# Local attention in six layers: a new order of the TensorE, ScalarE, VectorE and GpSimd steps of a turn

## What is computed

```
for i in range(6):
    q, k, v = split(shift_tokens(x) @ Wqkv[i])              # 16 heads of 64
    q, k = rotary(l2norm(q) * qs), rotary(l2norm(k) * ks)
    sim = q @ k^T * 8, windows of 32 tokens, each looks at itself and the one before
    x = x + (softmax(sim) @ v) @ Wo[i]
    a, gate = split(layernorm(shift_tokens(x)) @ W1[i] + b1[i])
    x = x + (a * gelu(gate)) @ W2[i] + b2[i]
```

## Time and profile before

| what | value |
|---|---|
| median of 3 runs | 2087.13 us (2086.69 to 2090.17) |
| profiled execution, its own time | 2087.44 us |
| its span, first to last instruction | 2085.6 us |
| TensorE busy | 1895.0 us, 91% of the span |
| GpSimd busy | 1445.9 us, 69% |
| VectorE busy | 1446.0 us, 69% |
| ScalarE busy | 1395.4 us, 67% |

### The profile page before, as it was taken

How to read it: one execution, slowest core, us unless ns; L and a number is a source line. 1 busy time by engine, 2 the same in 40 slices (tenths; PEclk the granted TensorE clock), 3 DMA queues, 4 the chain that set the end, 5 groups by cost and what they waited for, 6 DMA issues and landing times. The chain is left out here.

```text
span 2085.6 us, 77661 instructions
## 1 busy us (share of the span) xinstructions
PE 1895.0 (91%) x32069; PEld 1312.6 (63%) x32069; DVE 1446.0 (69%) x2609; ACT 1395.4 (67%) x2781; POOL 1445.9 (69%) x1837
## 2 busy tenths in 40 slices
PE   5648999999999999999999999999999999669958
PEld 4526666666666666666666666666666666456648
DVE  2357687778776877777777867787778786245546
ACT  1157777787777777777777777777787777235425
POOL 1158887888788878887788778877888787112334
PEclk9779999999999999999999999999999999769969
DMA  2011131111311113111113111121111111030002
GB/s 96 0 34 48 48 96 45 46 48 46 95 46 48 46 46 96 48 48 55 40 41 102 55 40 36 41 81 31 30 33 31 30 30 33 2 99 1 18 30 76
DMA packets 67088, 99.85 MB, mean 48 GB/s; under 512 B 15367, under 2 KB 51608, under 8 KB 65970
## 3 DMA queue, kind: packets, MB, share of 16 engines
q1 hardware_dynamic: 65234, 91.72, 15.3%
q0 software_dynamic: 1504, 3.17, 0.4%
HBM read 44.50 MB, written 21.45 MB: 32 GB/s over the span
## 5 line engine op out<-in xcount | busy, mean ns | idle before, releaser
L1074 PE MATMUL b_bank_proj<-layer_weights,b_stream_t 128*128 128x512 f32 x1152 | 589.4, 613 | 34.0 <-DVE b_plain_moved L948 17.9
L948 DVE TENSOR_TENSOR b_plain_moved<-b_bank_proj,b_rope 128x1024 f32<-128x1024 f32 x384 | 464.0, 1219 | 191.8 <-ACT b_squares L834 137.8
L759 POOL TENSOR_TENSOR b_rotated<-b_plain_moved 128x1024 f32<-128x1024 f32 x192 | 453.5, 2362 | 23.1 <-DVE b_plain_moved L948 18.7
L774 POOL TENSOR_TENSOR b_rotated<-b_rotated,b_inv_norm 128x1024 f32<-128x1024 f32 x192 | 365.2, 1902 | 15.6
L834 ACT ACTIVATE b_squares<-b_bank_proj 128x512 f32<-128x512 f32 x384 | 229.1, 597 | 116.1 <-PE b_bank_proj L1074 111.6
L865 ACT ACTIVATE b_k_t<-b_bank_shared 64x512 f32<-64x512 f32 x384 | 226.5, 590 | 119.9 <-PE b_bank_shared L1082 117.4
L1074 PEld LDWEIGHTS b_bank_proj<-layer_weights,b_stream_t 128*128 128x128 f32 x1152 | 186.9, 192 | 136.1 <-issue 45.7
L779 POOL TENSOR_TENSOR b_probs<-b_probs,b_inv_sum 128x512 f32<-128x512 f32 x192 | 200.3, 1044 | 90.1 <-DVE b_inv_sum L969 88.7
L856 ACT ACTIVATE b_q_t<-b_bank_shared 64x512 f32<-64x512 f32 x384 | 225.7, 588 | 34.3 <-PE b_bank_shared L1082 31.4
L1082 PE MATMUL b_bank_shared<-const_tables,b_rotated 128*128 128x128 f32 x1536 | 233.1, 277 | 15.6 <-POOL b_rotated L774 15.2
L1101 PEld LDWEIGHTS b_bank_scores<-b_k_t,b_q_t 128*32 128x32 f32 x12288 | 184.5, 111 | 98.9 <-issue 95.8
(11 more groups left out here) (320 smaller groups left out, 2866.8 us busy)
## 6 DMA issues: line engine op xcount, KB each, us to landing
b_v_shifted<-b_v SPq DMA_DIRECT2D x96, 384.0 KB, 3.5
sorted_rows<-constants SPq DMA_DIRECT2D x135, 129.0 KB, 3.4
layer_weights<-L_ffn_Wqkv SPq DMA_DIRECT2D x6, 1536.0 KB
b_v_shifted<-b_v SPq DMA_DIRECT2D x72, 128.0 KB, 3.4
layer_weights<-L_ffn_w SPq DMA_DIRECT2D x16, 256.0 KB, 5.2
layer_weights<-L_ffn_Wo SPq DMA_DIRECT2D x6, 512.0 KB
c_sorted_in<-sorted_rows SPq DMA_DIRECT2D x23, 129.0 KB, 2.1
layer_weights<-L_ffn_W SPq DMA_DIRECT2D x6, 341.0 KB
```

Of the source, the lines that this page charges most:

```text
L759: nc.gpsimd.tensor_tensor(out=turned[:, k, :], in0=pm[:, k, 0, :], in1=pm[:, k, 1, :], op=ALU.add).then_inc(add_done, 1)
L774: nc.gpsimd.tensor_tensor(out=tk, in0=tk, in1=repeat_last(rn[:, k, :], DH), op=ALU.mult).then_inc(rope_done, 1)
L948: nc.vector.tensor_tensor(to, src.to_broadcast(shape), tab.to_broadcast(shape), ALU.mult).then_inc(mul_done, 1)
L1074: nc.tensor.matmul(out, xs[:, b, t * P:(t + 1) * P], w, start=True, stop=True).then_inc(proj_full, 1)
```

## The change

All four lists are replaced; no code outside them differs. Over the 24 turns each engine does the same steps as before. Counted over the whole walk, no step of TensorE or ScalarE moves by more than five places, none of VectorE by more than three, none of GpSimd by more than two. The lists are also cut at another place of the turn, which alone moves nothing. From the diff (TensorE's list, and the stretches of the others that matter):

```
 PE_TURN
-    ("project", 1, 4), ("project", 1, 5), ("scores", 0, 0), ("probs_t", -1, 1), ("project", 2, 0),
-    ("project", 2, 1), ("pv", -1, 0), ("heads_t", 1, 0), ("project", 2, 2), ("heads_t", 1, 1), ("scores", 0, 1),
-    ("leave", -2, 0), ("project", 2, 3), ("out", -1, 0), ("heads_t", 1, 2), ("heads_t", 1, 3), ("back", -1, 0),
-    ("project", 2, 4), ("project", 2, 5), ("probs_t", 0, 0), ("scores", 1, 0), ("project", 3, 0),
-    ("heads_t", 2, 0), ("project", 3, 1), ("probs_t", 0, 1), ("scores", 1, 1), ("project", 3, 2), ("pv", 0, 0),
-    ("heads_t", 2, 1), ("norm_t", -1, 0), ("project", 3, 3), ("heads_t", 2, 2), ("up", -1, 0), ("heads_t", 2, 3),
-    ("out", 0, 0), ("up", -1, 1), ("enter", 1, 0), ("probs_t", 1, 0), ("scores", 2, 0), ("up", -1, 2),
-    ("up", -1, 3), ("project", 3, 4), ("probs_t", 1, 1), ("project", 3, 5), ("heads_t", 3, 0), ("project", 4, 0),
-    ("project", 4, 1), ("pv", 1, 0), ("heads_t", 3, 1), ("project", 4, 2), ("scores", 2, 1), ("out", 1, 0),
+    ("project", 2, 0), ("project", 2, 1), ("heads_t", 1, 0), ("probs_t", -1, 1), ("scores", 0, 0), ("pv", -1, 0),
+    ("heads_t", 1, 1), ("project", 2, 2), ("scores", 0, 1), ("project", 2, 3), ("heads_t", 1, 2), ("leave", -2, 0),
+    ("out", -1, 0), ("project", 2, 4), ("heads_t", 1, 3), ("project", 2, 5), ("back", -1, 0), ("project", 3, 0),
+    ("probs_t", 0, 0), ("scores", 1, 0), ("heads_t", 2, 0), ("probs_t", 0, 1), ("project", 3, 1), ("pv", 0, 0),
+    ("scores", 1, 1), ("project", 3, 2), ("heads_t", 2, 1), ("project", 3, 3), ("norm_t", -1, 0),
+    ("heads_t", 2, 2), ("enter", 1, 0), ("up", -1, 0), ("probs_t", 1, 0), ("up", -1, 1), ("out", 0, 0),
+    ("up", -1, 2), ("heads_t", 2, 3), ("up", -1, 3), ("project", 3, 4), ("scores", 2, 0), ("project", 3, 5),
+    ("project", 4, 0), ("probs_t", 1, 1), ("project", 4, 1), ("scores", 2, 1), ("heads_t", 3, 0),
+    ("project", 4, 2), ("pv", 1, 0), ("heads_t", 3, 1), ("up", -1, 4), ("heads_t", 3, 2), ("heads_t", 3, 3),
...
 ACT_TURN
-    ("heads_t", 2, 3), ("gelu", -1, 0), ("probs_t", 1, 0), ("gelu", -1, 1), ("enter", 1, 0), ("gelu", -1, 2),
-    ("root", 3, 1), ("project", 3, 4), ("probs_t", 1, 1), ("project", 3, 5), ("project", 4, 0), ("project", 4, 1),
+    ("heads_t", 2, 1), ("project", 3, 3), ("exp", 1, 1), ("heads_t", 2, 2), ("root", 3, 0), ("gelu", -1, 0),
+    ("enter", 1, 0), ("gelu", -1, 1), ("gelu", -1, 2), ("heads_t", 2, 3), ("root", 3, 1), ("project", 3, 4),
+    ("probs_t", 1, 0), ("project", 3, 5), ("exp", 2, 0), ("project", 4, 0), ("probs_t", 1, 1), ("project", 4, 1),
...
 DVE_TURN  (one tile: mul, soft, norms in their order)
-    ("norms", 5, 1), ("residual", 2, 0), ("soft", 4, 0), ("mul", 6, 0), ("norms", 6, 0), ("mul", 6, 1),
+    ("down", -1, 0), ("norms", 5, 1), ("residual", 2, 0), ("mul", 6, 0), ("soft", 4, 0), ("norms", 6, 0),
+    ("mul", 6, 1), ("share", 4, 0), ("soft", 4, 1), ("mul", 6, 2), ("mul", 6, 3), ("residual", 3, 0),
...
 POOL_TURN  (around the first tile of a turn)
-    ("rope", -1, 1), ("clamp", 0, 0), ("weigh", -2, 0), ("add", 0, 0), ("rope", 0, 0), ("weigh", -2, 1),
+    ("clamp", 0, 0), ("rope", -1, 1), ("weigh", -2, 0), ("add", 0, 0), ("rope", 0, 0), ("weigh", -2, 1),
```

More of the change, by code:

```diff
@@ L501 @@
-    ("project", 4, 1), ("pv", 1, 0), ("heads_t", 3, 1), ("project", 4, 2), ("scores", 2, 1), ("out", 1, 0),
-    ("heads_t", 3, 2), ("up", -1, 4), ("up", -1, 5), ("probs_t", 2, 0), ("heads_t", 3, 3), ("project", 4, 3),
-    ("project", 4, 4), ("scores", 3, 0), ("probs_t", 2, 1), ("heads_t", 4, 0), ("project", 4, 5),
+    ("project", 0, 5), ("heads_t", 0, 0), ("scores", -1, 1), ("probs_t", -2, 1), ("project", 1, 0),
+    ("project", 1, 1), ("pv", -2, 0), ("project", 1, 2), ("heads_t", 0, 1), ("down", -2, 0), ("project", 1, 3),
@@ new lines @@
+    ("heads_t", 0, 2), ("out", -2, 0), ("project", 1, 4), ("project", 1, 5), ("heads_t", 0, 3), ("probs_t", -1, 0),
+    ("project", 2, 0), ("project", 2, 1), ("heads_t", 1, 0), ("probs_t", -1, 1), ("scores", 0, 0), ("pv", -1, 0),
+    ("heads_t", 1, 1), ("project", 2, 2), ("scores", 0, 1), ("project", 2, 3), ("heads_t", 1, 2), ("leave", -2, 0),
+    ("out", -1, 0), ("project", 2, 4), ("heads_t", 1, 3), ("project", 2, 5), ("back", -1, 0), ("project", 3, 0),
+    ("probs_t", 0, 0), ("scores", 1, 0), ("heads_t", 2, 0), ("probs_t", 0, 1), ("project", 3, 1), ("pv", 0, 0),
@@ L504 @@
+    ("up", -1, 5), ("out", 1, 0), ("project", 4, 3), ("project", 4, 4), ("scores", 3, 0), ("probs_t", 2, 0),
 ]
 ACT_TURN = [
[L508 to L511, removed]
@@ L517 @@
[L517 to L521, removed]
+    ("attended", -2, 1), ("heads_t", 0, 1), ("project", 1, 3), ("heads_t", 0, 2), ("root", 1, 0),
@@ new lines @@
+    ("project", 1, 4), ("project", 1, 5), ("heads_t", 0, 3), ("probs_t", -1, 0), ("project", 2, 0), ("root", 1, 1),
+    ("probs_t", -1, 1), ("heads_t", 1, 0), ("project", 2, 1), ("exp", 0, 0), ("attended", -1, 0),
+    ("project", 2, 2), ("root", 2, 0), ("attended", -1, 1), ("project", 2, 3), ("heads_t", 1, 1),
+    ("heads_t", 1, 2), ("exp", 0, 1), ("project", 2, 4), ("leave", -2, 0), ("heads_t", 1, 3), ("back", -1, 0),
+    ("probs_t", 0, 0), ("project", 2, 5), ("project", 3, 0), ("probs_t", 0, 1), ("project", 3, 1), ("exp", 1, 0),
@@ new lines @@
+    ("root", 2, 1), ("attended", 0, 0), ("heads_t", 2, 0), ("attended", 0, 1), ("project", 3, 2),
+    ("heads_t", 2, 1), ("project", 3, 3), ("exp", 1, 1), ("heads_t", 2, 2), ("root", 3, 0), ("gelu", -1, 0),
+    ("enter", 1, 0), ("gelu", -1, 1), ("gelu", -1, 2), ("heads_t", 2, 3), ("root", 3, 1), ("project", 3, 4),
+    ("probs_t", 1, 0), ("project", 3, 5), ("exp", 2, 0), ("project", 4, 0), ("probs_t", 1, 1), ("project", 4, 1),
+    ("heads_t", 3, 0), ("root", 4, 0), ("project", 4, 2), ("attended", 1, 0), ("attended", 1, 1),
@@ L522 @@
+    ("heads_t", 3, 1), ("heads_t", 3, 2), ("heads_t", 3, 3), ("project", 4, 3), ("project", 4, 4), ("exp", 2, 1),
+    ("probs_t", 2, 0), ("project", 4, 5), ("heads_t", 4, 0), ("probs_t", 2, 1), ("project", 5, 0), ("root", 4, 1),
+    ("project", 5, 1), ("exp", 3, 0), ("exp", 3, 1), ("project", 5, 2), ("attended", 2, 0),
 ]
 DVE_TURN = [
-    ("residual", 0, 0), ("hidden", -1, 0), ("mul", 4, 0), ("norms", 4, 0), ("share", 2, 0), ("mul", 4, 1),
-    ("mul", 4, 2), ("soft", 2, 1), ("hidden", -1, 1), ("hidden", -1, 2), ("residual", 1, 0), ("share", 2, 1),
@@ L533 @@
-    ("mul", 7, 1), ("mul", 7, 2), ("scale", 0, 0), ("soft", 5, 1), ("mul", 7, 3), ("share", 5, 1), ("norms", 7, 1),
-    ("soft", 6, 0),
+    ("norms", 3, 1), ("hidden", -1, 0), ("soft", 2, 0), ("mul", 4, 0), ("norms", 4, 0), ("residual", 0, 0),
+    ("mul", 4, 1), ("mul", 4, 2), ("share", 2, 0), ("hidden", -1, 1), ("hidden", -1, 2), ("soft", 2, 1),
+    ("residual", 1, 0), ("mul", 4, 3), ("share", 2, 1), ("norms", 4, 1), ("soft", 3, 0), ("soft", 3, 1),
+    ("mul", 5, 0), ("norms", 5, 0), ("share", 3, 0), ("mul", 5, 1), ("share", 3, 1), ("mul", 5, 2), ("mul", 5, 3),
@@ L535 @@
+    ("down", -1, 0), ("norms", 5, 1), ("residual", 2, 0), ("mul", 6, 0), ("soft", 4, 0), ("norms", 6, 0),
+    ("mul", 6, 1), ("share", 4, 0), ("soft", 4, 1), ("mul", 6, 2), ("mul", 6, 3), ("residual", 3, 0),
+    ("share", 4, 1), ("norms", 6, 1), ("stats", 0, 0), ("soft", 5, 0), ("mul", 7, 0), ("norms", 7, 0),
+    ("mul", 7, 1), ("share", 5, 0), ("soft", 5, 1), ("mul", 7, 2), ("scale", 0, 0), ("mul", 7, 3), ("share", 5, 1),
 ]
 POOL_TURN = [
-    ("add", -2, 1), ("clamp", -2, 1), ("weigh", -4, 1), ("rstd", -2, 0), ("rope", -2, 1), ("clamp", -1, 0),
+    ("add", -3, 1), ("rope", -3, 1), ("clamp", -2, 0), ("add", -2, 0), ("weigh", -4, 0), ("rope", -2, 0),
@@ L540 @@
+    ("weigh", -4, 1), ("add", -2, 1), ("clamp", -2, 1), ("rstd", -2, 0), ("rope", -2, 1), ("clamp", -1, 0),
     ("weigh", -3, 0), ("add", -1, 0), ("weigh", -3, 1), ("clamp", -1, 1), ("rope", -1, 0), ("add", -1, 1),
[L541 to L543 removed]
@@ L544 @@
-    ("weigh", 0, 0), ("rope", 2, 0),
+    ("clamp", 0, 0), ("rope", -1, 1), ("weigh", -2, 0), ("add", 0, 0), ("rope", 0, 0), ("weigh", -2, 1),
+    ("clamp", 0, 1), ("add", 0, 1), ("rope", 0, 1), ("weigh", -1, 0), ("clamp", 1, 0), ("add", 1, 0),
+    ("weigh", -1, 1), ("rope", 1, 0), ("clamp", 1, 1),
 ]
```

9 lines of the change are left out of this document (removed).

## The result

| | before | after |
|---|---|---|
| median | 2086.91 us (4 runs, 2084.05 to 2090.17) | 2165.15 us (4 runs, 2162.48 to 2170.81) |
| ratio, 95% interval | | 1.0378, 1.0351 to 1.0405: slower by 78 us |
| profiled execution, its span | 2087.44, 2085.6 | 2167.10, 2165.3 |
| turns 1 to 22 | 1507.7 us, 68.5 each | 1590.1 us, 72.3 each |
| stretches at half clock in turns 1 to 22 | 4, 14 us in all | 16, 58 us in all |

The account below looks back on a forecast made before the run. TensorE was taken as the bound; turns 1 to 22 summed to 12 x 70.2 (late blocks) + 10 x 68.2 + 5 x 0.3 = 1525.9 against 1507.7 us, 18 more on 2087.4: forecast 2106 us, range 2080 to 2125.

Parts of the forecast that it names:

- The bound and the reading of the gaps: TensorE bounds; gaps stand where 256-instruction blocks end; turn 11 borders at 148 of pv(-1,0) and 27 of scores(1,1).
- The price of a late block: A 256-instruction block wholly inside pv and scores side by side makes the next late by 1.6 us, bounds 0 to 2.2.
- The number of late blocks: Borders drift 6 to 10 instructions a turn and leave both pairs after 10 to 17 turns; 12 taken.
- The clock: Rival: clock falls at two new 1.6 us idles a turn, adding 38 us, 2144; chance 0.04.
- a clock below 1.00 inside turns: Sign that the forecast is wrong: TensorE's granted clock dropping within turns.
- The waits at up: up(1) waits 0.4 for VectorE's mul(3,3) in late-block turns; up(4) finds its bank 0.4 late through mul(4,2).
- heads_t(2,3) behind the table load: ScalarE makes these copies behind gelu(2) and the load, so scores(2,0) waits 1.3 us in every turn.
- GpSimd's chain: rope(2,1) ends at 56.7, so heads_t(2,2) waits 1.6 us a turn, swallowed where blocks are late.
- Layer's start: Rotary table 3.1 us earlier by clamp(0,0) ahead of rope(-1,1): 4 us at five layers, 20 us, 0.3 each left.
- steps at nominal distance: TensorE's own steps without waits: 64.75 us a turn, 0.5 less than before through fewer runs.
- hops and the rest: Semaphore hops, 0.15 us a turn.

Follow-up runs that it names:

- a_shift88: Changed kernel with 44 real transposes into an unused bank behind enter(0), once, 88 instructions more on TensorE: 2137.6 us, ratio 1.0222.
- a_noshift: Changed kernel with both copies of the shifted V cut from 1024 columns to 64: 2139.8 us, ratio 1.0236.
- a_gelu: Changed kernel with heads_t(2,3) ahead of the gelus on ScalarE and behind up(0) on TensorE: 2171.76 us, ratio 1.0416.
- b_pool: Kernel before with one exchange on GpSimd, clamp(0,0) (holds the rotary table) ahead of rope(-1,1): 2082.87 us, ratio 0.9974.

## Why the prediction was wrong, by its own steps

- **The bound and the reading of the gaps: right.** Blocks of 256, borders that wander three products a turn, and their places in turn 11, within 4 instructions of 148 and 27. a_shift88 confirms them by moving them. The Trainium skill (Advanced Engine Details and Errata, "ISA Cache") has lines of 256 instructions and two lines. With the 256 the trace agrees, in the borders; with the two lines it doesn't clash, since a block is late behind a short one, but no run counts them. It states no time for a line, and that is what had to be measured.
- **The price of a late block: the step that failed first.** "I take **1.6**, near turn 11's gap", between bounds of 0 and 2.2. Over the timeline of turns 1 to 22, pv(-1,0) lost 28.5 us in 19 turns (1.5 each), but scores(1,1) 31.6 in 15 (2.1 each); single gaps there reach 2.4, over the upper bound. Part of the difference are the copies of the shifted V (a_noshift), which the prediction had costed at nothing but their landing.
- **The number of late blocks: the step that failed next.** "I take 12" from 10 to 17 turns. The drift was 6 instructions a turn, the lower end: the three or four waits more that were counted from the code did not add to it. And a border that leaves scores(1,1) downward lands in pv(0,0) behind product 110, where the block still holds nearly only the pair: 11.6 us in turns 16 to 20. Together the late blocks cost 28.5 + 31.6 + 11.6 = 71.7 us, 39 of them; the forecast had 12 x 3.2 = 38.4 for 24. That is 33 too little.
- **The clock: a rival with a chance of 0.04 that came true in part.** "Against: 1.45 us idle at 221 left it at 1.00". That row was no rule: in the changed kernel it fell behind 1.04 us at 940.5. 16 stretches, nearly all of 3.4 us; steps in them took 27.4 us over nominal, for which the sum had nothing. The prediction had itself named a clock below 1.00 inside turns as a sign of being wrong.
- **The waits at up: the wrong one.** The sum had 0.4 at up(1) for mul in the 12 turns with late blocks and 0.4 at up(4) in every turn, 13.6 us in all. In the run up(0) waits for VectorE's scale, 12.1 us in 21 turns (0.8 a turn as a distance), and up(4) for mul only 2.2 us.
- **heads_t(2,3) behind the table load: right.** 1.28 us in each turn, as a distance, for 1.3. The next activation came 1.30 us behind the load's start (971.78 and 973.08); the drain that the Trainium skill states (ScalarE: Activation LUTs, "What ACT_TABLE_LOAD costs") is not in this trace either. That the wait was there did not mean that it cost its sum (a_gelu).
- **GpSimd's chain: right as a mechanism, and too much in the sum.** In a_shift88 heads_t(2,2) waits 1.35 us for rope in each of 13 turns (1.6 said); where blocks are late it waits hardly at all. The forecast had ten turns of that, 16 us; the changed kernel, with late blocks in nearly every turn, has 1.9. Turns without late blocks were to take 68.2; turns 11 to 20 of a_shift88, which still hold a few, take 69.0.
- **Layer's start: right in the result.** VectorE's wait for the table went, and the clock's drops behind it. What b_pool adds is that the same exchange alone, in the order of before, is worth 4 to 5 us and not 20, since probs_t pays for it in the other turns.

Turns 1 to 22 were forecast at 1525.9 us and took 1590.1, 64.2 more. By the prediction's own terms:

| | forecast | measured |
|---|---|---|
| steps at nominal distance | 1424.5 | 1424.8 |
| gaps inside runs | 38.4 | 74.5 |
| pauses between steps: scores(2,0) 28.6, rope 16, up 13.6, layers' starts 1.5 | 59.7 | 54.1 |
| steps at half clock | 0 | 27.4 |
| hops and the rest | 3.3 | 9.3 |

The measured column takes the account of the 82 us above, from 22 x 65.25 us for the order before; the rest is what then remains. So the two steps on late blocks failed by 36 us (33 in the three steps above, the rest in runs for which the forecast had none) and the clock by 27, while the pauses came out 6 us under their sum, two errors of it against each other: 14 too much for rope, 8 or so too little elsewhere.

## What to carry to other kernels

On an engine fed with thousands of tiny instructions the stream itself is a resource: count instructions against time, and keep a longer step between two dense runs, above all where a block's border can fall. Price an idle with the clock that it may bring down, and with any second wait that follows it closely, and check a reordering for the bank or buffer that each step then inherits. A step that is needed rarely (here the table, once in four turns) is better cut up into the idle places of its engine long before it is due than moved to the front of the critical turn.
